# A macaron transformer block: normalisation moved from VectorE to ScalarE in both eight-expert layers, and parts of the first steps reordered

## What is computed

```python
def _layernorm(x, axis=-1, eps=1e-05):
    m = jnp.mean(x, axis=axis, keepdims=True)
    v = jnp.var(x, axis=axis, keepdims=True)
    return (x - m) / jnp.sqrt(v + eps)

def _L0_ffn_ref(x, Wg, Wu, Wd, Wr, temperature):
    weights = _routing_weights(x, Wr, temperature)   # 8 weights per token
    gate = jnp.einsum('btd,edi->beti', x, Wg)
    up = jnp.einsum('btd,edi->beti', x, Wu)
    h = jax.nn.silu(gate) * up
    e_out = jnp.einsum('beti,eid->betd', h, Wd)
    out = jnp.einsum('bte,betd->btd', weights, e_out)
    return out

x = x + 0.5 * _L0_ffn_ref(_layernorm(x, axis=-1), L0_ffn_Wg, L0_ffn_Wu, L0_ffn_Wd, L0_ffn_Wr, L0_ffn_temperature)
x = x + _L0_attn_ref(_layernorm(x, axis=-1), L0_attn_w_qkv, L0_attn_w_proj)
```

## Time and profile before

| | |
|---|---|
| three executions | 923.75, 927.27 and 927.50 us; median 927.27 |
| profiled execution | 923.53 us, of which the span of the core's instructions is 922.3 us |
| TensorE, its weight loads | 755.3 us (82%), 616.0 us (67%) |
| VectorE | 546.8 us (59%) |
| ScalarE | 427.9 us (46%) |
| GpSimd | 494.6 us (54%) |
| mean granted TensorE clock | 0.925 of full |
| chain that ended last | PE 43%, DVE 19%, POOL 19%, issue 11%, ACT 4%, DMA 3% |

### The profile page before, as it was taken

How to read it: one execution, slowest core, us unless ns; L and a number is a source line. 1 busy time by engine, 2 the same in 40 slices (tenths; PEclk the granted TensorE clock), 3 DMA queues, 4 the chain that set the end, 5 groups by cost and what they waited for, 6 DMA issues and landing times.

```text
span 922.3 us, 18791 instructions
## 1 busy us (share of the span) xinstructions
PE 755.3 (82%) x6384; PEld 616.0 (67%) x6384; DVE 546.8 (59%) x1655; ACT 427.9 (46%) x1099; POOL 494.6 (54%) x488
## 2 busy tenths in 40 slices
PE   6899988889999998878998899915988997999600
PEld 5778755579967777767776788813666775888500
DVE  5974585668677758878873444401977662454205
ACT  3567646556145545555521666620454322666500
POOL 5555540016283024655673577776347772677773
PEclk9999979999889999999999999966998999999955
DMA  9999999900050041001112544314101113444216
GB/s 228 220 216 216 215 219 216 209 6 4 4 160 23 1 129 32 2 32 35 48 57 75 136 123 125 102 52 168 43 26 53 55 58 89 122 124 124 72 51 233
DMA packets 125757, 94.67 MB, mean 103 GB/s; under 512 B 10624, under 2 KB 116480, under 8 KB 125664
## 3 DMA queue, kind: packets, MB, share of 16 engines
q1 hardware_dynamic: 113472, 71.19, 33.7%
q0 software_dynamic: 10176, 21.65, 6.8%
q10 hardware_dynamic: 2016, 0.63, 0.3%
HBM read 34.05 MB, written 59.38 MB: 101 GB/s over the span
## 4 chain that ended last, share of the span: by engine, by line
PE 43%; DVE 19%; POOL 19%; issue 11%; ACT 4%; DMA 3%; SPq 0%; POOLq 0%; DVEq 0%; ACTq 0%
POOL expert_rows L677 10%; POOL sorted_rows L445 8%; PE banks L1638 5%; PE banks L1110 4%; PE banks L1685 3%; PE banks L1667 3%; PE banks L783 2%; PE banks L396 2%; PE banks L397 2%; PE banks L398 2%; DVE h L744 2%; PE banks L793 2%; ACT sg L691 2%; PE banks L785 2%; PE banks L784 2%
## 5 line engine op out<-in xcount | busy, mean ns | idle before, releaser
L677 POOL DMA_INDIRECT expert_rows<-y,goal x190 | 182.0, 958 | 92.8 <-issue 53.1
L445 POOL DMA_INDIRECT sorted_rows<-rows_x,row_of x128 | 127.1, 993 | 67.4 <-issue 37.2
L990 ACT ACTIVATE ys<-banks,wtab 128x128 f32<-128x128 f32 x256 | 73.0, 369 | 66.4 <-PE banks L1110 55.9
L744 DVE TENSOR_TENSOR h<-sg,banks 128x512 f32<-128x512 f32 x48 | 33.0, 688 | 97.3 <-ACT sg L691 95.2
L396 PE MATMUL banks<-x_high,w_high 128*128 128x512 f32 x192 | 86.4, 450 | 0.4 <-POOL w_low L880 0.4
L1110 PE MATMUL banks<-w,hT 128*128 128x128 f32 x512 | 73.5, 288 | 13.1 <-DVE hT L1031 12.7
L1110 PEld LDWEIGHTS banks<-w,hT 128*128 128x128 f32 x512 | 66.9, 198 | 21.9 <-DVE hT L1031 19.4
L915 POOL TENSOR_TENSOR x<-ys,x 128x512 f32<-128x512 f32 x44 | 56.2, 1277 | 46.7 <-ACT ys L990 46.2
L398 PE MATMUL banks<-x_high,w_low 128*128 128x512 f32 x192 | 77.8, 405 | 0.0
L397 PE MATMUL banks<-x_low,w_high 128*128 128x512 f32 x192 | 77.5, 404 | 0.0
L204 POOL TENSOR_TENSOR rstd<-rstd,mhalf 128x4 f32<-128x4 f32 x24 | 25.6, 1067 | 82.9 <-DVE rstd L198 82.6
(11 more groups left out here) (300 smaller groups left out, 1899.6 us busy)
## 6 DMA issues: line engine op xcount, KB each, us to landing
sorted_rows<-zeros SPq DMA_DIRECT2D x32, 1120.0 KB, 17.0
tile<-sorted_rows SPq DMA_DIRECT2D x192, 70.0 KB
routed_low<-in_ffn_w SPq DMA_DIRECT2D x8, 512.0 KB, 3.9
w<-in_ffn_w SPq DMA_DIRECT2D x20, 192.0 KB, 3.6
expert_rows<-y,goal POOLq DMA_INDIRECT x190
routed_down<-in_ffn_w SPq DMA_DIRECT2D x8, 256.0 KB, 5.4
sorted_rows<-rows_x,row_of POOLq DMA_INDIRECT x128
xnT<-expert_rows SPq DMA_DIRECT2D x2, 1024.0 KB, 5.6
```

The lines of the kernel that those rows point to most:

```text
L445: POOL.indirect_dma_start(sorted_rows, bass.IndirectOffsetOnAxis(self.row_of[:, g, i:i + 1], 0), rows_x[:, 4 * g + i % 4, :], None).then_i ...
L677: POOL.indirect_dma_start(expert_rows, bass.IndirectOffsetOnAxis(goal[:, 4 * q + i:4 * q + i + 1], 0), y[q % 6][:, i * P:(i + 1) * P], Non ...
L990: last = SCL.mul(ys[s % 2][:, j * P:(j + 1) * P], bank[4 + s % 2][:, j * P:(j + 1) * P], wtab[:, t, e:e + 1])
```

## The change

- A new instruction on VectorE, `Norm.shifted(g)`, makes -mean x rstd for a group's four tiles (128x4), and a new ScalarE function, `Norm.scalar_normalise(g)`, makes the normalised rows as four `Identity` activations with scale rstd and bias shift. They take the place of `normalise(g)` in both calls of `ffn0`, in the norm for the landmark attention (groups 0 to 2 inside the first `ffn0`, group 3 in `attn0`), and in the sorted layer's norm inside the second `ffn0`. `attn1` keeps `normalise`.
- On ScalarE the normalisations of groups 0 and 1 stand ahead of the layer's first copy, those of groups 2 and 3 at the end of steps 3 and 5, those of the following norms at the end of their step, behind `scale`.
- Groups 2 and 3: statistics in steps 1 and 3 (before: ahead of step 0, and step 1), power in POOL's steps 2 and 4 (before: ahead of step 0, and step 0), shift in steps 3 and 5 (`normalise` stood in 2 and 3), transposes in 5 and 6 (3 and 4), copy in 6 and 7 (4 and 5), logits, split and low in 7 and 8 (5 and 6).
- The route of groups 2 and 3: read and powers in step 9, cubes and zone in 10, best and two in 11, weights in 12 (before: 7, 8, 8, 9, 10, 10, 11); its ScalarE part in step 9 (7).
- In the first layer the casts of expert weights 4 to 7 stand in steps 1 and 2 on ScalarE and POOL (before 0 and 1).

```diff
+            def shifted(self, g):
+
+                ts = slice(4 * g, 4 * g + 4)
+                DVE.wait_ge(*rstd_ready(self.first + g + 1))
+                DVE.scalar_tensor_tensor(out=shift[:, ts], in0=mv[:, ts, 0], scalar=-1.0, in1=rstd[:, ts], op0=ALU.mult,
+                                         op1=ALU.mult).then_inc(*shift_ready.inc)
+
+            def scalar_normalise(self, g):
+                SCL.wait_ge(*shift_ready(self.first + g + 1))
+                if self.first:
+                    SCL.wait_ge(*norms[self.first // NG - 1].transposed(g))
+                for t in range(4 * g, 4 * g + 4):
+                    last = SCL.activation(xn[:, t, :], x[:, t, :], ACT.Identity, scale=rstd[:, t:t + 1], bias=shift[:, t:t + 1])
                 last.then_inc(*xn_ready.inc)
...
+            parts_at = {1: (4, 5), 2: (6, 7)} if first else {0: (0, 1), 1: (2, 3), 6: (4, 5), 7: (6, 7)}
...
                 low(0)
                 if first:
-                    low_part(fresh[0], 0)
-                    low_part(fresh[1], 1)
-                norm.power(2)
-                if first:
-                    low_part(fresh[2], 2)
-                    low_part(fresh[3], 3)
-                low_parts = {0: (4, 5), 1: (6, 7)} if first else {0: (0, 1), 1: (2, 3), 6: (4, 5), 7: (6, 7)}
+                    for i in range(4):
+                        low_part(fresh[i], i)
                 for s in range(POOL_ADDS):
-                    for i in low_parts.get(s, ()):
+                    for i in parts_at.get(s, ()):
                         low_part(fresh[i], i)
-                    if s == 0:
-                        norm.power(3)
+                    if s in (2, 4):
+                        norm.power(s // 2 + 1)
                     add(POOL, s)
-                    if s in (2, 5, 6):
-                        low({2: 1, 5: 2, 6: 3}[s])
+                    if s in (2, 7, 8):
+                        low({2: 1, 7: 2, 8: 3}[s])
...
+                norm.scalar_normalise(0)
+                norm.scalar_normalise(1)
                 norm.copy(0)
...
-                    if s in (4, 5):
-                        norm.copy(s - 2)
+                    if s in (6, 7):
+                        norm.copy(s - 4)
...
-                    if s in (2, 7):
-                        FFN0.scalar_route((s + 3) // 5)
+                    if s in (2, 9):
+                        FFN0.scalar_route(1 if s == 2 else 2)
+                    if s in (3, 5):
+                        norm.scalar_normalise(s // 2 + 1)
+                    for g in following_at(s, "normalised"):
+                        following.scalar_normalise(g)
+                    for g in groups_at(s, "normalised"):
+                        srt.norm.scalar_normalise(g)
...
                 routes = [FFN0.route(n) for n in range(3)]
-                assert next(routes[0]) == "read"
-                norm.statistics(2, updated[2])
-                for piece in ("powers", "cubes"):
+                for piece in ("read", "powers", "cubes"):
                     assert next(routes[0]) == piece
                 routed_at = {0: ((0, "zone"), (0, "best"), (0, "two")), 1: ((0, "weights"),), 2: ((1, "read"),), 3: ((1, "powers"),),
-                             4: ((1, "cubes"), (1, "zone")), 5: ((1, "best"),), 6: ((1, "two"),), 7: ((1, "weights"), (2, "read")),
-                             8: ((2, "powers"), (2, "cubes")), 9: ((2, "zone"),), 10: ((2, "best"), (2, "two")), 11: ((2, "weights"),)}
+                             4: ((1, "cubes"), (1, "zone")), 5: ((1, "best"),), 6: ((1, "two"),), 7: ((1, "weights"),),
+                             9: ((2, "read"), (2, "powers")), 10: ((2, "cubes"), (2, "zone")), 11: ((2, "best"), (2, "two")), 12: ((2, "weights"),)}
...
-                    if s == 1:
-                        norm.statistics(3, updated[3])
-                    if s in (2, 3):
-                        norm.normalise(s)
-                    if s in (1, 5, 6):
-                        split({1: 1, 5: 2, 6: 3}[s])
+                    if s in (1, 3):
+                        norm.statistics(s // 2 + 2, updated[s // 2 + 2])
+                    if s in (3, 5):
+                        norm.shifted(s // 2 + 1)
+                    if s in (1, 7, 8):
+                        split({1: 1, 7: 2, 8: 3}[s])
...
-                    if s in (3, 4):
-                        norm.transposes(s - 1)
-                    if s in (1, 5, 6):
-                        FFN0.logits({1: 1, 5: 2, 6: 3}[s], norm)
+                    if s in (5, 6):
+                        norm.transposes(s - 3)
+                    if s in (1, 7, 8):
+                        FFN0.logits({1: 1, 7: 2, 8: 3}[s], norm)
...
                 for b in range(B):
+                    if b == 1:
+                        norm.scalar_normalise(NG - 1)
                     if b == 2:
                         norm.copy(NG - 1)
...
                 evict_k(0)
-                norm.normalise(NG - 1)
+                norm.shifted(NG - 1)
                 evict_k(1)
```

More of the change, by code:

```diff
@@ L180, in build @@
         xT_transposed, xT_ready = signal("xT_transposed"), signal("xT_ready")
+        shift_ready = signal("shift_ready")
+        shift = sb("shift", [P, NT])
         class Norm:
@@ L211, in normalise @@
                     last = DVE.tensor_scalar(xn[:, t, :], x[:, t, :], mv[:, t, 0:1], rstd[:, t:t + 1], ALU.subtract, ALU.mult)
+                last.then_inc(*xn_ready.inc)
+            def shifted(self, g):
[9 more added lines that the diff above has]
+                    last = SCL.activation(xn[:, t, :], x[:, t, :], ACT.Identity, scale=rstd[:, t:t + 1], bias=shift[:, t:t + 1])
                 last.then_inc(*xn_ready.inc)
@@ L451, in vector_group @@
                 yield "variance"
-                self.norm.normalise(g)
+                if self.another:
+                    self.norm.shifted(g)
+                else:
+                    self.norm.normalise(g)
                 yield "normalised"
@@ L978, in scalar_engine @@
                     high_part(fresh[3], 3)
-                high_parts = {0: (4, 5), 1: (6, 7)} if first else {0: (0, 1), 1: (2, 3), 6: (4, 5), 7: (6, 7)}
                 def scale(s):
@@ L1000, in scalar_engine @@
                         srt.scalar_shared(s)
-                    for i in high_parts.get(s, ()):
+                    for i in parts_at.get(s, ()):
                         high_part(fresh[i], i)
-                    if s in (4, 5):
-                        norm.copy(s - 2)
+                    if s in (6, 7):
+                        norm.copy(s - 4)
                     for g in following_at(s, "copy"):
@@ L1034, in vector_engine @@
                 norm.statistics(1, updated[1])
-                norm.normalise(0)
+                norm.shifted(0)
                 if first:
@@ L1081, in vector_engine @@
                     for g in following_at(s, "normalised"):
-                        following.normalise(g)
+                        following.shifted(g)
                 if srt:
```

2 lines of the change are left out of this document (1 added, 1 removed).

## The result

| | kernel before | changed kernel |
|---|---|---|
| median, us (4 runs each) | 927.38 (923.75 to 930.34) | 942.17 (941.29 to 943.28) |
| profiled execution, us (span) | 923.53 (922.3) | 941.37 (939.9) |
| granted clock over the span | 0.925 | 0.920 |

The change makes the kernel 1.7% slower: ratio 1.0171, 95% interval 1.0142 to 1.0200. The forecast was 929.5, and its range ended at 936.5.

A forecast was written before the change was run, and what follows sets the result against it. VectorE was taken as the late engine in steps 0 to 11 of both expert layers. First layer +2.4, first attention layer -0.8, second layer +2.7 gave +4.3 on 925.4: 929.5 us, 8 in 10 range 919.5 to 936.5.

The forecast's parts named there:

- The price of a normalisation: Four Identity activations on ScalarE for one group: taken as 1.2 us, bounds 1.1 and 1.5.
- rival B: Slower: silu behind ScalarE's normalisation is late in every group, also in the steady stretch; +10, 935.5 us, chance 0.20.
- Start of the first layer: Normalising groups 0 and 1 on ScalarE ahead of the first copy delays the first product: +1.9 us.
- Step 3 to 4: First layer: silu(4) queues behind the normalisation, 6.7 us against 5.9; `hidden(4)` still starts 0.9 us earlier.
- Steps 5 to 8: First layer: two groups of transposes move here, +1.3; `normalise(3)` at step 5 is covered; `down(8)` +0.3 us.
- Step 9: First layer: read and powers in one step, VectorE standing about 3.5 us between them; `down(10)` 1.5 us earlier.
- Step 12: First layer: weights, shift, normalise, silu(13) take 4.9 us against 3.1 of TensorE work; `down(13)` 1.8 us late.
- First attention layer: VectorE's four normalising instructions become one of 0.2 us, and the key eviction and landmark sums move up: -0.8 us.
- Second layer: Second expert layer, its start, steps, later routes and sorted groups summed: +2.7 us.
- The signs: The forecast would be wrong if silu(4) isn't held, or if VectorE is idle in steps 10 to 12.
- C: Tables: Identity in another set than Silu, so each of 12 normalisations costs two loads; over +25, 950 us, chance 0.02.
- A: Faster: VectorE's relief wins in steps 3, 4, 9 and 12, two slow stretches vanish; -5.0, 920.4 us, chance 0.25.

The follow-up runs named there:

- e16: Kernel before, old order, with all 16 groups normalised on ScalarE, from step 3 on behind the next step's silu: 927.36 us, ratio 0.9953 to the kernel before.
- e3: Kernel before with only first-layer weight casts 4 to 7 and the third group's statistics and power moved later: 926.27 us, ratio 1.0009.
- e4: Changed kernel with every ScalarE normalisation from step 3 on moved behind the next step's silu: 936.21 us, ratio 1.0122 to the kernel before.
- e2: Changed kernel's order with all normalisations on VectorE, the moves alone: 929.31 us, ratio 1.0035 to the kernel before.
- e5: Changed kernel with the second route's powers in step 10 instead of 9 (zone to 11, two to 12): 942.02 us, ratio 1.0156 to the kernel before.
- e1: Kernel before's order with all 16 groups normalised on ScalarE ahead of silu, the swap alone: 938.27 us, ratio 1.0135 to the kernel before.
- e12: Changed kernel with the next layer's four groups and the four sorted groups back on VectorE: 938.41 us, ratio 1.0145 to the kernel before.
- e13: Kernel before with the third and fourth groups of each expert layer normalised on ScalarE behind the silu of steps 3 and 4: 920.84 us, ratio 0.9943.
- e7: Changed kernel with normalisations from step 3 on behind the next silu and the second route's powers in step 10: 931.30 us, ratio 1.0055 to the kernel before.
- e9: New order, second route's powers in step 10, only each expert layer's third and fourth groups on ScalarE, behind silu: 931.54 us, ratio 1.0069 to the kernel before.
- e14: Kernel before with the third and fourth groups of each expert layer on ScalarE, ahead of the silu of steps 3 and 4: 928.06 us, ratio 1.0011.
- e11: Changed kernel with four extra ScalarE Identity instructions behind the second group's normalisation, into an unread tile, for their durations only: one execution 943.42 us.

## Why the prediction was wrong, step by step

**The price of a normalisation was mis-sized.** I took 1.2 us for a group, bounds 1.1 and 1.5; it is 1.65. The error is in the choice of the row: four scalings in 1.14 us read one pointer, this form two. Even 4 x 0.369, offered as an upper bound, lay below it, as it had nothing for the second pointer. With 1.65 rival B's own condition, over 1.3 us, was met, and B gave 935.5, still 6.7 us short. The price alone is not what made the kernel slower: e16 pays it for all 16 groups and is faster than the kernel before.

**Start of the first layer.** +1.9 for the first product, +3.6 measured: 3.17 us instead of 2.4, and TensorE, after 1.8 us of waiting, needs 1.85 us for eight small logits and 0.77 for its first product. Still `hidden(0)` was only 0.05 late, and `hidden(3)` at 28.57 between my 27.5 and the old 29.20. That the waits for the loads go was right; e3 shows that what this gives is only lent.

**Step 3 to 4.** I had 6.7 us against 5.9, it took 7.39: lead +0.87, not -0.9. The mechanism was the one named, silu(4) behind the normalisation, and TensorE waited 4.82 us for `hidden(4)` (over 3 was foreseen). Missing were 0.45 in the normalisation and 0.6 in `shifted`, which took 1.29 us beside GpSimd.

**Steps 5 to 8.** "`normalise(3)` at step 5 is covered" was the step that failed outright. I asked when ScalarE is free (37.4) and not when `shift` comes: it stands behind zone, `hidden(5)` and best on VectorE, at 41.38, so silu(6) ended at 43.71 and not near 39.5, and the lead at step 6 was +3.68. In both layers this was made good by step 9 (-1.5, where e4 has -1.1; in the second, counted from its step 0, -1.3 and -1.6). So what it spoilt by itself is the forecast of this step. The same question, what `shift` itself stands behind, was not asked at the later groups either, and there the loss lasted.

**Step 9.** Down(10) was to be 1.5 us earlier; `hidden(10)` is 3.5 us later than before. I had the wait of 3.5 us (2.66 measured behind the read), but the powers, taken at 1.4, took 3.05 (54.26 to 57.31), with L329 1.21 instead of 0.2. From step 9 to 10 the lead grows by 5.0 us, in e2 too (-5.1 to -0.1): this is the order's part, and not the swap's. By e5, though, mending this step alone gives nothing that can be measured.

**Step 12.** A delay of 1.8 us (4.9 - 3.1) was foreseen, 2.4 is measured (4.40 to 6.81), by the chain named. The sum then took this delay as the whole lead at step 13 and dropped the -1.5 of step 9; carried on, the first layer would have come to +0.9, further off still. So the first layer: +2.4 foreseen, about +7 measured.

**First attention layer.** -0.8 foreseen, -0.1 at the first maximum. ScalarE's normalisation, at 119.16 us, waits 1.84 us for `shift` ahead of the second query eviction. That this ate the gain is argued.

**Second layer.** +2.7 foreseen, +5.9 measured beyond its step 0; e2 has 0.2 of it and e1 5.3. The 2.3 us for routes that come later cost nothing lasting: e2 is 2.1 us further behind at step 13 than at step 0, and 0.2 at the end. What failed is the price of the swapped groups, each with its wait for `shift` ahead of a silu (22.1 us in seven waits). I had put the sorted ones at +0.4, -0.2 and +0.3, and steps 3 and 4 at -0.5. Against e4, with the same work behind silu, the change is level at step 9, 2.5 us further behind at step 10, where the first sorted group's normalisation stands ahead of silu(10), and 4.3 at the end (5.9 and 1.6). With the sorted and the next layer's groups back on VectorE (e12) 3.8 of the 5.9 are left. That step 10 in the changed kernel, ScalarE and then VectorE:

```profile
392.61 1.65 ACT L228 ACTIVATE rows_x<-x,shift,rstd 128x128 f32<-128x128 f32 x4 [2.38 <-DVE shift L220]
394.16 0.57 ACT L1017 ACTIVATE sg<-banks 128x512 f32<-128x512 f32 x1
...
392.41 0.16 DVE L220 SCALAR_TENSOR_TENSOR shift<-mv,rstd 128x4 f32<-128x4 f32 x1
394.77 0.69 DVE L1056 TENSOR_TENSOR hT<-sg,banks 128x512 f32<-128x512 f32 x1 [2.19 <-ACT sg L1017]
```

The forecast had such a group as 1.3 us of VectorE's work against 1.2 and 0.6 us of ScalarE's, nearly even, and left out that VectorE would stand idle 2.19 us for the silu behind it.

**The signs.** Of what was to show the forecast wrong nothing came: silu(4) was held, and VectorE was busy in steps 10 to 12. These signs asked whether the mechanism was there and not what it costs.

**The rivals.** B names the true mechanism, with the wrong place: it had the cost in the steady stretch, where "nothing is made good". There, in the first layer, two steps were 1.5 us late and both were made good; the cost arose at the start, in steps 3 to 13, and in the second layer, where e1 and e4 show it. C is out: the traces have five table loads before and five after. The Trainium skill, "ScalarE: Activation LUTs", section "Table sets: the hidden batching unit", has identity in every set, and the trace agrees. A's relief exists, and e13 has it: 0.57%. The change spends it on the place.

**Order and swap don't add where the swap is well placed.** The order costs 0.35% with VectorE alone (e2), 0.36% on top of e1, but 1.7% on top of e16 (e4). This fits the leads: from step 9 to 15 the new order loses 6 to 8 us in every version (e2 6.8, e4 6.7, e7 6.2, e9 5.9, the change 8.3), the old order next to nothing (e13 0.0, e16 -0.2). With VectorE alone the new order has earned 5.1 us by step 9 to pay this with; with ScalarE normalising behind silu the old order has already earned 2.4 to 4.5 of it, and the new one adds little. That these are the same microseconds is argued from the leads and was not tried by itself.

## What to carry to other kernels

When work moves to another engine, look up what it waits for and what stands behind it there: an instruction that waits for engine V, placed ahead of the one that V waits for, makes the two engines take turns. Here that cost 1.4 to 1.6 us for each group so placed (17 us for twelve groups, e1 against e16, and 6.3 for four, e14 against e13), about as much as the 1.65 us of work itself. Price a form by a row with the same operands, or bound it above that row. A stall removed in a stretch where another engine is full may be only lent: read the lead again ten steps later.

## What the runs showed of the hardware

A ScalarE instruction on 128 columns pays 92 to 94 ns for each scale or bias that it reads from SBUF (292, 384, 478 ns in e11), more than the 54 ns that 64 columns cost.

A `shifted` of four elements takes 0.16 us at 41.38 us of the changed kernel, where GpSimd is idle, and 1.29 at 32.47, beside an instruction of GpSimd: that one ends at 33.74 and `shifted` at 33.76. At 67.07, beside an add, it takes 1.24. The Trainium skill, "SBUF — State Buffer", section "Who interferes with whom", has it that a VectorE instruction with two SBUF inputs contends with a GpSimd instruction that reads SBUF, since its second input comes through a read interface that they share. The trace agrees, and both sizes are those of the prediction, 0.2 and 1.2.

After a wait of 4.82 us TensorE's granted clock is 0.50 for 4.5 us, after one of 3.66 us (at 59.50) again 0.50 for 4.5. At that level the same products, from the down products to the next transposes, take 1.8 us more (4.44 against 2.60), where the prediction had 1.4 for a slow stretch.

The stretch between the two expert layers took 243.3 us in one profile and 240.2 in another, with the same code and on the same chip (e13, e14), and 249.5 on another chip (e16, with three of its normalisations on ScalarE). A few microseconds of difference between two profiles over such a stretch say nothing of a change.
